# A graph kernel's four gathers on one semaphore, and range tables loaded with bounds checks

## The reference, cut to what matters

```python
# four convolutions, each:
h = x @ W
msg = h[src] * norm[:, None]
out = jax.ops.segment_sum(msg, dst, num_segments=n_nodes) + b
# two attention layers, each:
att = jnp.einsum('ehd,ehd->eh', q[dst], k[src]) / scale
ex = jnp.exp(att - m[dst])
alpha = ex / (s[dst] + 1e-16)
aggr = jax.ops.segment_sum((v[src] * alpha[:, :, None]).reshape(-1, D), dst, num_segments=n)
```

## Time and profile before

| what | value |
|---|---|
| median of three runs | 8635.9 us |
| the profiled execution: span from its first to its last instruction | 8638.3 us |
| passes 0, 1, 2, 3 (between the first range loads of each) | 1262, 1271, 1286, 1217 us |
| passes 4, 5 | 1705, 1679 us |
| busy | PE 57%, POOL 54%, DVE 45%, ACT 7% |
| mean granted TensorE clock | 0.745 |
| gathers (L1154) | 4704, of 977 ns each |
| range loads (L353) | 150 on DVE, 150 on PE, 50 on ACT |

### The profile page before, as it was taken

The page is one execution under the profiler, slowest core; times in us unless marked ns, Lnnn a source line. Parts: engine busy times, 40 slices in busy tenths (PEclk is TensorE's granted clock), DMA queues, the critical chain, the costliest instruction groups (busy, mean ns, idle before and its releaser), DMA issues.

```text
span 8638.3 us, 111062 instructions
## 1 busy us (share of the span) xinstructions
PE 4901.2 (57%) x23425; PEld 3838.8 (44%) x23426; DVE 3919.4 (45%) x10474; ACT 605.2 (7%) x1438; POOL 4642.4 (54%) x4895
## 2 busy tenths in 40 slices
PE   2345565455565556665344455666676755666666
PEld 1234444334443334554233343455555644555555
DVE  8124566123344123443123344555566645555665
ACT  0000000000000000000000000001111210011111
POOL 0666664666554666654666664554443345544442
PEclk9755555668787677887556676787888877787787
DMA  2111111333222333221111113333332233333331
GB/s 53 47 45 48 50 49 47 90 88 92 86 87 71 90 88 87 84 80 53 45 45 49 50 53 90 113 107 97 94 94 86 73 95 111 109 96 93 91 87 55
DMA packets 312486, 662.67 MB, mean 77 GB/s; under 512 B 85049, under 2 KB 134216, under 8 KB 312386
## 3 DMA queue, kind: packets, MB, share of 16 engines
q0 software_dynamic: 200704, 514.10, 21.3%
q1 hardware_dynamic: 64590, 111.62, 4.4%
q10 hardware_dynamic: 47092, 35.73, 1.3%
HBM read 625.40 MB, written 35.72 MB: 77 GB/s over the span
## 4 chain that ended last, share of the span: by engine, by line
another core or an unknown queue 28%; PE 24%; DVE 22%; issue 15%; DVEq 7%; ACT 2%; DMA 1%; SPq 0%; POOL 0%; ACTq 0%; POOLq 0%
PE acc_ps L1491 12%; PE acc_ps L1441 3%; PE q_ps L1431 3%; DVE masks L585 3%; DVE dots L776 2%; DVE wide L773 2%; DVEq L585 2%; DVE early L443 2%; DVE masks L605 1%; PE q_ps L1412 1%; DVE rs_y L396 1%; DVEq L353 1%; DVE rs_t L394 1%; PE bank L1520 1%
## 5 line engine op out<-in xcount | busy, mean ns | idle before, releaser
L1154 POOL DMA_INDIRECT ring<-rows,idx_stage x4704 | 4596.9, 977 | 3437.6 <-issue 1693.9
L1491 PE MATMUL acc_ps<-ring,masks 128*128 x7808 | 2102.2, 431 | 1973.0 <-DVE masks L585 1553.3
L1491 PEld LDWEIGHTS acc_ps<-ring,masks 128*128 128x128 f32 x7808 | 1637.0, 261 | 2407.1 <-issue 2257.8
L585 DVE SCALAR_TENSOR_TENSOR masks<-dst_f,neg_first,lane 128x256 f32<-128x256 f32 x1952 | 899.0, 484 | 2850.0 <-remote 1731.2
L1431 PE MATMUL q_ps<-own,conv_only 128*128 (+1 forms) x3904 | 758.2, 363 | 833.4 <-DVE conv_only L593 576.6
L1431 PEld LDWEIGHTS q_ps<-own,conv_only 128*128 128x128 f32 x3904 | 678.8, 265 | 895.0 <-issue 891.0
L1441 PE MATMUL acc_ps<-msg,masks 128*128 x3904 | 665.5, 323 | 357.4 <-DVE msg L788 322.8
L1441 PEld LDWEIGHTS acc_ps<-msg,masks 128*128 128x128 f32 x3904 | 612.9, 228 | 474.2 <-issue 462.6
L605 DVE SCALAR_TENSOR_TENSOR masks<-dst_f,neg_first,lane 128x512 f32<-128x512 f32 x488 | 366.5, 751 | 591.8 <-remote 395.8
L1412 PE MATMUL q_ps<-bias_rows,zeros_bf 128*128 128x512 bf16 x1450 | 446.2, 448 | 0.0
L593 DVE TENSOR_SCALAR conv_only<-conv_only,node_id 128x512 f32 x488 | 240.4, 493 | 329.6 <-remote 175.8
(11 more groups left out here) (201 smaller groups left out, 3718.2 us busy)
## 6 DMA issues: line engine op xcount, KB each, us to landing
conv_only<-dst_rows SPq DMA_DIRECT2D x394, 256.0 KB
ring<-rows,idx_stage POOLq DMA_INDIRECT x4704
rows<-own ACTq DMA_DIRECT2D x48, 256.0 KB
rows<-wide ACTq DMA_DIRECT2D x48, 256.0 KB
rows<-own ACTq DMA_DIRECT2D x26, 128.0 KB
rows<-own ACTq DMA_DIRECT2D x1, 3136.0 KB
out<-own ACTq DMA_DIRECT2D x24, 128.0 KB
w_ff<-in_L_gnn_W SPq DMA_DIRECT2D x4, 256.0 KB
```

The lines of the kernel that those rows point to most:

```text
L585: return vec.scalar_tensor_tensor(out=to, in0=dst_f[:, bass.ds(col + 2 * h, 2)].unsqueeze(2).broadcast_to([P, 2, P]), scalar=neg_first[:, ...
L1154: pool.indirect_dma_start(ring[:, j, 0:WIDTH[p]], None, tables[p][:, :], bass.IndirectOffsetOnAxis(ap=idx_stage[:, half, j:j + 1], axis=0) ...
L1491: ins = pe.matmul(to, masks[:, u, j, :], rhs, start=False, stop=final and j == GC - 1)
```

## The change

Each group of four gathers gets one semaphore, which its four DMAs raise together by 64. SP waits for it once, in the instruction that raises `group_landed`. And `pair_range` no longer passes the argument that leaves out the check of the loaded values' bounds, so each of the eight values is checked to lie from 0 to `MAX_SEQ` after the load.

```diff
-        landed = [sem(f"landed_{j}") for j in range(RING)]
+        landed = [sem(f"landed_{q}") for q in range(RG)]
...
             _, r = nc.values_load_multi_w_load_instructions(
-                ranges[0:1, bass.ds(s * 2, 2), :].rearrange("a t c -> a (t c)"), [engine], min_val=0, max_val=MAX_SEQ,
-                skip_runtime_bounds_check_because="the table is computed from counts of the edges")
+                ranges[0:1, bass.ds(s * 2, 2), :].rearrange("a t c -> a (t c)"), [engine], min_val=0, max_val=MAX_SEQ)
...
                         for q in range(RG):
-                            for j in range(q * GC, (q + 1) * GC):
-                                sp.wait_ge(landed[j], count * 16)
+                            sp.wait_ge(landed[q], count * (16 * GC))
                             sp.sem_inc(group_landed, 1)
...
                             load_row(ahead, lap * RG + q + 1, (group + 1) & (DST_RING - 1))
-                            for j in range(q * GC, (q + 1) * GC):
-                                sp.wait_ge(landed[j], count * 16)
+                            sp.wait_ge(landed[q], count * (16 * GC))
                             sp.sem_inc(group_landed, 1)
...
-                                    ).then_inc(landed[j], 16)
+                                    ).then_inc(landed[q], 16)
```

## The result

The changed kernel took 8851.33 us (median of 4 runs, 8837.18 to 8876.48), the kernel before 8632.25 us (4 runs, 8628.16 to 8641.26). The ratio is 1.0255, with a 95% interval of 1.0229 to 1.0281: 219 us slower. The forecast was 8902 us, the range 8750 to 9040. The sign and the range held; of the 266 us in the sum 219 came, 47 fewer.

What follows compares the result with a forecast made beforehand. It took a ping-pong of DVE and PE to bound the kernel, with POOL's gathers and full-ring stops pacing convolutions. 124 + 12 + 130 = 266 us on a span of 8638.3, 2.4 above the median, gave 8902 us, range 8750 to 9040.

Steps and rivals of the forecast that it cites:

- The semaphore, taken at 0: SP's single wait per gather group: 0 us, since other groups in the ring hide it; bound of -70 us.
- one of my signs of being wrong: The prediction is wrong if the waits for `group_landed` turn out to have been on the path.
- the bound: SP saves 0.06 us per group; if every one of 1176 groups were awaited, 70 us gained.
- The size of a check: On DVE's sequencer behind the range load: 0.34 us a check, 2.7 us a load, 403 us for 150 loads.
- Cheap checks: Rival, 13%: only a sequencer's first comparison costs 221 ns, later ones 71 ns; 8760 us.
- PE and ACT hidden: Checks on PE (2.2 us a load) and ACT cost nothing, as both idle for DVE, PE 3.92 us.
- Passes 4 and 5, full price, 130 us: PE idles for DVE's first mask behind the load, so 48 of 50 loads cost 2.7 us each.
- Passes 0 to 2, 124 us: Late frees delay POOL: 18 loads a pass at 2.0 us, last two 2.7, first five nothing; 41 us a pass.
- absorbed in the convolutions: Rival, 6%: unnamed waits take up the checks there; only passes 4 and 5 pay, 130 us; 8766 us.
- Pass 3, 12 us: DVE's 5.47 us wait for PE hides the checks; a third of the other convolutions' price, for steps without it.
- Full price: Rival, 13%: a convolution step goes by the chain, not POOL; each load costs 2.7 us everywhere, 9039 us.
- Larger loops: Rival, 2%: added checks make steps outgrow instruction memory; refetch stops add 170 us on top, 9070 us.

Runs made afterwards that it cites:

- condition B: Sets of runs in which the kernel before took 7231 or 7237 us; whether its chip differs from the other condition's is not known.
- condition A: Runs in which the kernel before took 8632 us (the forecast's case) or 8771 us (a later set).
- the first comparison: The changed kernel against the kernel before, ahead of the follow-up sets: 8851.33 against 8632.25 us, ratio 1.0255.
- The second dose on DVE: Changed kernel with each value checked twice on DVE, the second time against a limit one higher: 9216.7 us, against 8965.4 for the changed kernel.
- the step from four to eight checks: All eight values checked on DVE instead of four, eight on PE and ACT, old four semaphores: 227 against 129 us above the kernel before.
- The second dose on PE and ACT: Changed kernel with each value checked twice on PE and ACT, once on DVE: 9055.2 us, against 8965.4 for the changed kernel.
- half the checks: Only the first and last group of each tile checked, on all engines: 7344.3 us, 1.0152 of the kernel before.
- set 3: Third set of four kernels on one chip, kernel before at 7231 us: changed kernel 7461.9 us, with the gathers' old four semaphores 7465.5 us.

## Why the prediction was right, and where not

**The semaphore, taken at 0.** Shown in condition B: 3.6 us, within the spread of the runs. The reason that I gave, that PE hardly waits for a landed group, is wrong there, with 391 such waits; and that these waits turn out to be on the path was one of my signs of being wrong (in condition B POOL's gathers, which they wait for, are on the chain with 28%). What failed is the bound: an awaited group is not worth 0.06 us. In condition A, in which the forecast was made, it is not shown.

**The size of a check.** Forecast 0.34 us on DVE and 2.7 for a load; the median is 2.25 for a load, and in condition B the mean is 2.27. The single row of L579 was dearer than the 1200 that followed. "Cheap checks" fell: the comparison has a median of 183 ns, not 71. In the first comparison, in condition A, the mean was 2.65 us, so that 150 loads took 398 us of DVE's sequencer. That this is near the 403 forecast is luck: a check was taken too dear, and the stalls were not foreseen.

**PE and ACT hidden.** Mostly: 13 and 17% of an added dose is paid. So the cover of 3.92 us is probably not there at every load.

**Passes 4 and 5, full price, 130 us.** 133 us measured. The second dose on DVE was paid to 100% there, and so was the step from four to eight checks in condition B. DVE's first dose was 2.31 us x 50 = 116 us long, so some 18 of the 133 are not DVE's. The second dose on PE and ACT cost 24 us in these passes, which fits; their first was not measured in the first comparison. So the match is partly luck: 48 loads at 2.31 us are 111 us, and what I had taken at nothing for PE and ACT probably made up for it.

**Passes 0 to 2, 124 us.** The size is wrong, and by my own sign so is more: the prediction was to be wrong if these passes grow by under 20 us, and of 18, 15 and 30 us two are under it. The mechanism was a ring freed late, with a slack of POOL behind it that takes the first part of a dose. The step shown above and the 108 us of L634 bear it out, but no run takes the ring out of the way, and POOL's waits as a whole grew by 54 us where the four convolutions grew by 81. In condition B POOL hardly waits for DVE and the convolutions pay a part of a dose too, so the ring is not the only path. I had read 0.7 us of slack from one step. Over 54 steady loads, with the last two of each pass at the full 2.25, the 63 us leave (63 - 13.5) / 54 = 0.92 us a load. So 1.3 us of 2.25 was absorbed, and in the step shown above it was 1.1. The second dose, at 74%, shows that most of this slack is used up. Where the rest went is not shown. The unnamed waits of passes 1 and 2 shrank by 101 us, as the rival "absorbed in the convolutions" has it, but other parts of the chain changed as much.

**Pass 3, 12 us.** 18 measured. That the 5.47 us wait of the earlier trace rows covers most loads, but fewer than I took, would fit; it was not counted.

**The rivals.** "Full price" is out, since the convolutions paid 81 us of 282. "Larger loops" is out for its size: the instruction queue moved 52 packets against the 49 of the earlier trace rows, and half the checks cost about half (108 of 227 us). By the terms as they were measured, 0 + 63 + 18 + 133 = 214 us, which is the growth of the profiled span; the medians of all runs differ by 219.

The unnamed waits can be told in part. The largest group of them before, 266 waits and 1731 us ahead of DVE's masks at L585, is for `masks_used`, the semaphore that PE raises with its matmuls at L1491. Such a wait is unnamed because the update comes more than 1.5 us after the end that the profile gives for PE's raising instruction before it: in one case of pass 1 four updates come between 2119.07 and 2119.25 us, where PE's last matmul ends at 2107.94. In condition B they come with the matmul's end, and all of DVE's waits for it stand there under PE's name, 1981 us. What holds PE's signal back in condition A is open. Why checks cost as much in condition B, where POOL waits for DVE only 54 us in four passes, is settled by pass and not by path: it is the attention passes that pay in full, and what the convolutions pay there has no cause shown.

## What to carry to other kernels

A check of a loaded register took some 0.28 us here of the sequencer of the engine that loads it, so that a load of eight values with checks took nearly five times as long as without (2.85 us against 0.6). What it costs is read from the place: who waits for the first instruction behind the load, and what else would have come late anyway. Check only the values that need it, and check each as late as its first use, behind work that another engine waits for (two of DVE's four checks moved so took 52 of 108 us away); moving the checks as one block to another place may only move the wait. One step read from a trace suggests a mechanism, but a slack wants many steps, and a dose twice as large tells it too.

## What the runs showed of the hardware

One kernel, the changed one, took 7462 us in one set and 8965 us in another. The chain by engine, first of the changed kernel in the first comparison, then in set 3:

```profile
another core or an unknown queue 25%; PE 25%; DVE 22%; issue 16%; DVEq 10%; ACT 2%; SPq 0%; DMA 0%; ACTq 0%; POOL 0%; POOLq 0%
```

```profile
POOL 28%; PE 23%; DVE 19%; issue 19%; DVEq 7%; DMA 2%; ACT 2%; POOLq 1%; SPq 0%; ACTq 0%
```

In condition B there are no unnamed waits, and POOL's gathers are on the chain. The work of POOL and DVE is the same: 4704 gathers at 979 and 980 ns, DVE busy 3923 and 3936 us. PE is busy 4970 and 4716 us, at a mean granted clock of 0.736 and 0.799, which is little beside the 1396 us between the two spans. What else differs is the spread of small instructions. The row of set 3 beside the 4/183/710 above:

```profile
L353 DVEq FUSED_REGOPS  x1200: 183/183/224, 219.5 to 7396.8; - x172
```

And POOL hardly waits for DVE in the convolutions there. The view by line of passes 0 to 3, set 3:

```profile
L1151 POOL DMA_INDIRECT ring<-rows,idx_stage x3136 | 3066.7, 978 | 1173.7 <-issue 1108.2 <-DVEq L634 35.5 <-DVEq L624 18.2
```

That is 54 us, against the 865 us above. The third difference is in the traces themselves, which lack updates of semaphores in condition A: the changed kernel's has 1680 of `masks_used` for 1953 raising instructions, that of set 3 has 1949. The checks cost 231 us there and 219 and 195 us in condition A. What makes the two conditions is open.

The assertion takes 18 ns on PE and 23 on DVE, the comparison 146 and 183. The Trainium skill, in Runtime: NRT & Kernel Launch, section Instruction fetch mechanics, gives some 20 cycles as the floor of an instruction. By the estimate of the prediction, 0.3 us for 16 instructions, that is some 19 ns. The assertion is near such a floor and the comparison far above it; in condition A, single rows of both are also far below it, at 3 and 4 ns.
